# Graph convolutions on one core: node features as two 32-bit parts instead of three bf16 parts, edge counts stored as bytes and widened on chip

## The reference: what is computed

```
def _gcn_conv(x, src, dst, W, b, n_nodes):
    h = x @ W
    ...                       # self loops are added to src, dst as s, d
    deg = segment_sum(ones, d)
    dis = where(deg > 0, rsqrt(deg), 0.0)
    msg = h[s] * (dis[s] * dis[d])[:, None]
    return segment_sum(msg, d) + b

h = relu(batch_norm(gcn_conv(h, W1, b1)))
h = relu(batch_norm(gcn_conv(h, W2, b2)))
h = relu(gcn_conv(h, W3, b3))
h = gcn_conv(h, W3, b3)
x = x + h
```

## Time and profile before

| | |
|---|---|
| time, median of 3 runs | 3986.09 us |
| span of the profiled execution | 3987.6 us |
| PE busy | 3679.6 us (92%), 21902 matmul records |
| DVE busy | 2167.3 us (54%) |
| ACT busy | 1880.8 us (47%) |
| POOL busy | 1505.2 us (38%) |
| moved by DMA | 560.45 MB |

### The profile page before, as it was taken

How to read it: one execution, slowest core, us unless ns; L and a number is a source line. 1 busy time by engine, 2 the same in 40 slices (tenths; PEclk the granted TensorE clock), 3 DMA queues, 4 the chain that set the end, 5 groups by cost and what they waited for, 6 DMA issues and landing times. The chain is left out here.

```text
span 3987.6 us, 61840 instructions
## 1 busy us (share of the span) xinstructions
PE 3679.6 (92%) x21902; PEld 2157.9 (54%) x21902; DVE 2167.3 (54%) x3396; ACT 1880.8 (47%) x5147; POOL 1505.2 (38%) x1605
## 2 busy tenths in 40 slices
PE   5899999999999999999985879999999999999999
PEld 3566666666666666666653544445444544454444
DVE  8788888888888888888874750002100210012000
ACT  4788888888888888888863660002000100011000
POOL 2677777777777777777760000000000000000000
PEclk8788888888888888888886989999999999999999
DMA  6443333333333333333334126665666566665665
GB/s 202 128 109 104 105 106 105 105 106 105 106 105 105 106 106 106 105 106 105 105 92 88 38 65 204 204 196 181 199 194 208 174 194 203 205 189 184 213 204 159
DMA packets 467250, 560.45 MB, mean 141 GB/s; under 512 B 45449, under 2 KB 411684, under 8 KB 466686
## 3 DMA queue, kind: packets, MB, share of 16 engines
q1 hardware_dynamic: 383558, 366.63, 30.4%
q0 software_dynamic: 51168, 107.68, 12.2%
q10 hardware_dynamic: 32248, 82.62, 5.6%
HBM read 455.16 MB, written 103.20 MB: 140 GB/s over the span
## 5 line engine op out<-in xcount | busy, mean ns | idle before, releaser
L900 POOL DMA_INDIRECT fts<-ft_tab,src_all x1568 | 1483.0, 946 | 478.0 <-issue 477.4
L2171 PE MATMUL cv_acc<-cv_cnt,cv_parts 128*128 128x512 bf16 (+1 forms) x7056 | 1431.3, 366 | 0.0
L2171 PEld LDWEIGHTS cv_acc<-cv_cnt,cv_parts 128*128 128x128 bf16 x7056 | 666.0, 98 | 761.7
L2006 DVE TENSOR_TENSOR cv_y<-cv_acc,dis_row 128x512 f32<-128x512 f32 (+1 forms) x52 | 34.4, 661 | 1355.1 <-PE cv_acc L2171 1326.5
L937 DVE TENSOR_TENSOR ohk<-iota_ps,key_cols 128x784 bf16<-128x784 f32 x784 | 724.9, 966 | 6.1
L1030 ACT ACTIVATE dist_l<-lo_iota,low 128x128 bf16<-128x128 f16 x1960 | 593.7, 388 | 18.6 <-ACT low L1025 0.8
L1189 PE MATMUL agg_ps<-terms,oh 128*64 128x141 f32 x2744 | 528.7, 364 | 25.6 <-DVE terms L974 25.0
L1189 PEld LDWEIGHTS agg_ps<-terms,oh 128*64 128x64 f32 x2744 | 458.1, 180 | 80.6 <-DVE terms L974 67.3
L1082 ACT CAST strip<-adj_ps 128x392 bf16<-128x392 f32 x784 | 372.2, 475 | 271.4 <-PE adj_ps L1133 239.2
L1133 PE MATMUL adj_ps<-ohk,ohl 128*128 128x196 bf16 x3136 | 431.2, 263 | 0.0
L951 DVE TENSOR_TENSOR prod<-ftd_ps,fts 128x780 f32<-128x780 f32 (+1 forms) x392 | 271.1, 692 | 220.5 <-DMA fts<-ft_tab,src_all 212.3
(11 more groups left out here) (261 smaller groups left out, 2919.9 us busy)
## 6 DMA issues: line engine op xcount, KB each, us to landing
cv_cnt<-adj SPq DMA_DIRECT2D x96, 2048.0 KB, 8.3
cv_cnt<-adj SPq DMA_DIRECT2D x48, 2176.0 KB, 8.6
adj<-strip ACTq DMA_DIRECT2D x196, 392.0 KB
fts<-ft_tab,src_all POOLq DMA_INDIRECT x1568
win<-ft_tab SPq DMA_DIRECT2D x196, 65.0 KB
agg_tab<-res SPq DMA_DIRECT2D x196, 35.2 KB
cv_cnt<-adj SPq DMA_DIRECT2D x8, 512.0 KB, 3.7
agg_tab<-zero_f SPq DMA_DIRECT2D x10, 352.5 KB
```

Source lines behind the costliest of these rows:

```text
L900: nc.gpsimd.indirect_dma_start(fts[u][:, k, :], None, ft_tab[:, :], bass.IndirectOffsetOnAxis(src_all[:, n, k:k + 1], 0)).then_inc(gathere ...
L2171: last = nc.tensor.matmul(a[:, 0:width], parts[:, r, b, :], cnt[q][:, 0:width // SUB, (b - b0) * SUB:(b - b0 + 1) * SUB], start=(b == 0 an ...
```

## The change

1. The features are kept as two parts of type `float32r`, a 32-bit format that TensorE multiplies with 12 significant bits, so two parts carry 24 bits. The stationary operand of a source block is loaded twice, and there are 98 matmuls a group instead of 147.
2. Both operands of a matmul have this type, so the counts too are needed as 32-bit numbers. They are stored in `adj` as bytes, loaded as bytes (chunks of 15, 18 and 16 blocks), and widened in SBUF: of each unit of three blocks VectorE widens two (one cast of 1024 elements) and ScalarE the third (one of 512), into a ring of four units, `cv_ring`; the 49th block has a tile of its own, `cv_rest`, which ScalarE fills. TensorE waits for both engines at each unit and gives a unit back by `unit_used`.
3. In the first phase the scaling moves from ScalarE to VectorE, two instructions a tile of seven blocks (`scaled`), and there is one subtraction (`low`) where `split` had four instructions. ScalarE keeps `rectify` and makes the high part (`high`).
4. SyncE loads a chunk when the widening engines have read the one before, no longer when TensorE has. The ring of the next layer's first units is widened ahead of the last `finish_group` of a layer.
5. The loops over groups are written out in all layers.

```diff
-    adj = dram("adj", (NS, P, STRIP), BF16)
+    adj = dram("adj", (NS, P, STRIP), U8)
...
-        strip = sb("strip", [P, 2, NT, NA, HALF], BF16, c)
+        strip = sb("strip", [P, 2, NT, NA, HALF], U8, c)
...
+    UB = 3
+    UNITS = NT // UB
+    RING = 4
-        parts = sb("cv_parts", [P, 3, NT, D], BF16, c)
-        cnt = [g["cv_cnt0"]] + [sb(f"cv_cnt{q}", [P, SPG, CMAX * SUB], BF16, c) for q in (1, 2)]
+        parts = sb("cv_parts", [P, 2, NT, D], F32R, c)
+        cnt = [g["cv_cnt0"]] + [sb(f"cv_cnt{q}", [P, SPG, CHUNKS[q][1] * SUB], U8, c) for q in (1, 2)]
+        ring = sb("cv_ring", [P, RING, UB, GRP], F32R, c)
+        rest = sb("cv_rest", [P, GRP], F32R, c)
...
@@ SyncE
-                            sp.wait_ge(cnt_used[q], n + 1)
+                            if n:
+                                sp.wait_ge(s["wide_v"], unit_no(n - 1, (b0 + m) // UB))
+                                sp.wait_ge(s["wide_s"], (n - 1) * (UNITS + 1) + -(-(b0 + m) // UB))
...
@@ VectorE
+            def widen(n, u):
+                b = u * UB
+                dve.wait_ge(cnt_in[chunk_of(b)], 16 * (n + 1))
+                wait(dve, s["unit_used"], unit_no(n, u) - RING + 1)
+                src, view = widened(n, b, UB - 1)
+                nc.vector.tensor_copy(view(ring[:, u % RING, 0:UB - 1, :]), src).then_inc(s["wide_v"], 1)
...
+                    for i in range(1, NGA):
+                        for u in range(UNITS):
+                            if u == RING:
+                                finish_group(i - 1)
+                                if l == L - 1 and i >= 2:
+                                    add_rows(i - 2)
+                            widen(l * NGA + i, u)
+                    if l < L - 1:
+                        for u in range(RING):
+                            widen((l + 1) * NGA, u)
+                    finish_group(NGR)
...
@@ ScalarE
+            def widen(n, u):
+                b = u * UB + UB - 1
+                act.wait_ge(cnt_in[chunk_of(b)], 16 * (n + 1))
+                wait(act, s["unit_used"], unit_no(n, u) - RING + 1)
+                src, view = widened(n, b, 1)
+                nc.scalar.copy(view(ring[:, u % RING, UB - 1:UB, :]), src).then_inc(s["wide_s"], 1)
...
@@ TensorE
-                        for r in range(3):
-                            last = nc.tensor.matmul(a[:, 0:width], parts[:, r, b, :],
-                                                    cnt[q][:, 0:width // SUB, (b - b0) * SUB:(b - b0 + 1) * SUB],
-                                                    start=(b == 0 and r == 0), stop=(b == NT - 1 and r == 2))
+            def add_block(n, b):
+                u, w = b // UB, width(n % NGA)
+                if u < UNITS:
+                    if b % UB == 0:
+                        pe.wait_ge(s["wide_v"], unit_no(n, u) + 1)
+                    if b % UB == UB - 1:
+                        pe.wait_ge(s["wide_s"], n * (UNITS + 1) + u + 1)
+                    counts = ring[:, u % RING, b % UB, 0:w]
+                else:
+                    pe.wait_ge(s["wide_s"], (n + 1) * (UNITS + 1))
+                    counts = rest[:, 0:w]
+                for r in range(2):
+                    last = nc.tensor.matmul(acc[n % 2][:, 0:w], parts[:, r, b, :], counts,
+                                            start=(b == 0 and r == 0), stop=(b == NT - 1 and r == 1))
```

More of the change, by code:

```diff
@@ L7 @@
 BF16 = mybir.dt.bfloat16
+F32R = mybir.dt.float32r
+U8 = mybir.dt.uint8
 FP16 = mybir.dt.float16
@@ L2013, in _ @@
-                with dve.If(flag):
+                    dve.wait_ge(s["w_ps"], n + 1)
+                    if n >= 2:
+                        dve.wait_ge(s["high"], n - 1)
+                        dve.wait_ge(s["low"], n - 1)
+                    for b1 in range(0, w, 4):
+                        m = min(4, w - b1)
+                        last = nc.vector.tensor_tensor(
+                            hs[k % 2][:, b1:b1 + m, :], w_ps[k % 2][:, b1 // 4, 0:m * D].rearrange("p (b d) -> p b d", d=D),
+                            dis_col[:, b0 + b1:b0 + b1 + m].unsqueeze(2).to_broadcast([P, m, D]), ALU.mult)
@@ L2015, in _ @@
+                with dve.If(flag):
+                    scaled(0)
+                    for k in range(NW):
+                        if k + 1 < NW:
+                            scaled(k + 1)
+                        low(k)
+                    settle(dve, s["tick"])
                     with dve.Fori(0, NT) as k:
@@ L2063, in add_rows @@
                     def add_rows(n):
-                        w = GRP // P if n < NGR else LW // P
+                        w = width(n) // P
                         dve.wait_ge(s["out_ps"], n + 1)
@@ L2136, in _, with high, last_layer @@
-                in_turn(rectify, scaled)
+                def high(k):
+                    n, (b0, w) = l * NW + k, TILES[k]
+                    act.wait_ge(s["hs"], n + 1)
+                    nc.scalar.copy(parts[:, 0, b0:b0 + w, :], hs[k % 2][:, 0:w, :]).then_inc(s["high"], 1)
+                with act.If(flag):
+                    act.wait_ge(s["ready"], l + 1)
+                    for k in range(2):
+                        rectify(k)
+                    for k in range(NW):
+                        if k + 2 < NW:
+                            rectify(k + 2)
+                        high(k)
+                    if l == L - 1:
+                        act.wait_ge(s["y"], 2 * 7 + 2)
+                        act.sem_inc(s["out_ps"], 2)
+                        def last_layer(k, u):
+                            act.wait_ge(s["out_ps"], k + 1)
+                            nc.scalar.copy(stage[u][:].rearrange("f b p -> f (b p)"), hT[:, ds(k * BW, BW)]
+                                           ).then_inc(s["staged"], 1)
+                        with act.Fori(0, NB // 2) as m:
+                            for u in range(2):
+                                last_layer(2 * m + u, u)
+                        last_layer(NB - 1, 0)
@@ new lines, in _ @@
+                with act.Else():
+                    if l == 0:
+                        for u in range(RING):
+                            widen(0, u)
+                    act.wait_ge(s["ready"], l + 1)
+                    for k in range(2):
+                        rectify(k)
+                    for k in range(NW):
+                        if k + 2 < NW:
+                            rectify(k + 2)
+                        high(k)
+                        if k:
+                            for u in units_after(k - 1):
+                                widen(l * NGA, u)
+                    for u in units_after(NW - 1):
+                        widen(l * NGA, u)
+                    widen_rest(l * NGA)
+                    for i in range(1, NGA):
+                        for u in range(UNITS):
+                            widen(l * NGA + i, u)
+                        widen_rest(l * NGA + i)
+                    if l < L - 1:
+                        for u in range(RING):
+                            widen((l + 1) * NGA, u)
@@ L2176, in first_group, with group @@
+            def group(n):
+                wait(pe, acc_read, n - 1)
+                for b in range(NT):
+                    add_block(n, b)
             def first_group(l, k):
-                pe.wait_ge(s["split"], l * NW + k + 3)
+                if k == 0:
+                    wait(pe, acc_read, l * NGA - 1)
+                pe.wait_ge(s["low"], l * NW + k + 1)
                 for b in range(TILES[k][0], sum(TILES[k])):
-                    q = max(i for i in range(3) if CHUNKS[i][0] <= b)
-                    b0, m = CHUNKS[q]
-                    if b == b0:
-                        pe.wait_ge(cnt_in[q], (l * NGA + 1) * 16)
-                    for r in range(3):
-                        last = nc.tensor.matmul(acc[0][:], parts[:, r, b, :],
-                                                cnt[q][:, :, (b - b0) * SUB:(b - b0 + 1) * SUB],
-                                                start=(b == 0 and r == 0), stop=(b == NT - 1 and r == 2))
-                    if b == b0 + m - 1:
-                        last.then_inc(cnt_used[q], 1)
@@ L2218, in _ @@
                         settle(pe, s["tick_pe"])
-                        for r in range(3):
-                            last = nc.tensor.matmul(acc[0][:, 0:P], rows[:, r, :], oh[:], start=(r == 0), stop=(r == 2))
+                        for r in range(2):
+                            last = nc.tensor.matmul(acc[0][:, 0:P], rows[:, r, :], oh[:], start=(r == 0), stop=(r == 1))
                         last.then_inc(s["part_ps"], 1)
@@ L2247, in turn_rows @@
                             pe.wait_ge(s["sum"], n - 1)
-                        for b in range(w):
+                        for b in range(width(n) // P):
                             last = nc.tensor.transpose(w_ps[n % 2][:, 0, b * P:(b + 1) * P],
```

233 lines of the change are left out of this document (96 added, 137 removed).

## The result

| | before | after |
|---|---|---|
| median of 4 runs, same chip | 3986.83 us | 3559.27 us (3557.39 to 3560.38) |
| ratio | | 0.8924 (95%: 0.8912 to 0.8937) |
| profiled execution, span | 3987.6 us | 3557.1 us |

Faster by 428 us, where 495 was forecast (3491 us). The time is inside the range (3470 to 3580), and only 5 us from the time of a rival, VectorE as the bound (3564 us), so the number alone decides nothing. The trace does.

What follows compares the result with a forecast made beforehand. TensorE's matmul count times their distance was taken to bound the convolutions, gathers the attention stage. Middle groups -465, first groups -42, boundaries +10, layer 1 start +2.5 make -495 us: 3986 to 3491 us, range 3470 to 3580.

Steps and rivals of the forecast that it cites:

- VectorE as the bound: Rival, convolution groups: byte casts at the two-operand rate, 22.1 us a group on VectorE against 21.2; 3564 us, 24%.
- The mechanism: Convolutions: matmul count times distance is the time; 98 for 147 saves 10.57 us a group, -465 us in middle groups.
- The conditions under which a group fits: Middle groups: VectorE 13.4 us, ScalarE 10.5 us, ring returns and loads (6.2 us a chunk) fit within 21.2 us.
- two cycles a column: Rival, convolution matmuls: TensorE reads 32-bit columns at the f32 instruction's rate, 0.434 us a matmul; 4527 us, 9%.
- full f32: Rival, convolution matmuls: the type runs as two full f32 instructions, 85 us a group; over 6500 us, 2%.
- Bare weight loads: Rival, convolution matmuls: weight loads come out from under them, 0.216 + 0.19 us each, 39.8 us a group; 4386 us, 2%.
- The case that came true: Likeliest case, whole kernel: TensorE stays the bound of the convolutions; 3491 us, own range 3474 to 3525, 60%.
- the distance: Convolution matmuls of 512 columns: one instruction at one column a cycle, 0.216 us as for bf16, 21.2 us a group.
- The last group: Each layer's group of 128 columns: bounds 5.5 and 10.9 us, taken as 8.2 us, no gain.
- The boundary: Between layers: next layer's casts delay finish_group until 3.3 us after the sums are ready; +10 us for three.
- The starts of the layers: Start of each layer: shorter by a few instructions, at most 1.5 us each, not counted; layer 1 separately +2.5 us.
- the total for what is not a phase: Outside the phases: three boundaries, +10 us, and ScalarE's widening ahead of layer 1, +2.5 us; +12.5 us.

Runs made afterwards that it cites:

- experiment 1: Changed kernel with four layer 1 groups altered: 256 + 256 columns, 384 + 128, 320 + 192, and full f32; 3627.0 us.
- experiment 4: Changed kernel with VectorE widening each unit twice, first into a scratch tile as bf16; 3618.03 us, ratio 0.9078 to the kernel before.
- experiment 2: Changed kernel with FP16 in place of float32r for parts, ring and rest (22 bits); 3495.76 us, ratio 0.8769 to the kernel before.
- experiment 3: Changed kernel with TensorE's 98 unrolled matmuls in the skipped branch put back into a loop; 3542.45 us, ratio 0.8884 to the kernel before.
- experiment 9: Changed kernel with two layer 1 groups using 64 columns of the stationary part, or 64 partitions, for most source blocks; 3559.38 us.
- experiment 8: Changed kernel (float32r) with a loop in the skipped branch and the next layer's four casts moved into its first phase; 3541.11 us, ratio 0.8885.
- experiment 7: Changed kernel with FP16 parts, a loop in the skipped branch and the next layer's four casts moved into its first phase; 3469.78 us, ratio 0.8710.

## Why the prediction was right, and what it mis-sized

**The mechanism was right.** 98 matmuls for 147 on the engine that bounds the convolutions, one column a cycle, TensorE in the chain, the widening hidden. The conditions under which a group fits held with their numbers: casts of 0.693 and 0.623 us, chunks landing in 5.5 to 6.2 us, DMA share 0.52 to 0.54 for 0.55, attention unchanged. Of the rivals, two cycles a column (0.434 us) and full f32 (0.868) are refuted by the 0.227 us, full f32 besides by the 83.9 us of experiment 1. Bare weight loads (0.41 us) are refuted as well: 188 ns of load lie within the 227. On VectorE as the bound, experiment 4 decides.

That the range holds the time is in part luck. The case that came true had a range of its own, 3474 to 3525 us, and 3559 lies above it; the stated range reaches to 3580 only for the sake of the VectorE rival, which did not happen.

**The failed step is the distance.** "I take one instruction at one column a cycle, 0.216 us" took over the whole bf16 distance, the columns and what stands beside them. The columns were right; what stands beside them is 13.3 ns for float32r (512 and 256 columns, experiment 1) and 2.5 for bf16. In numbers: 48 groups x (22.26 - 21.16) = 53 us of the 68 that are missing. The forecast had a range for its likeliest case up to 3525 and in it no term for this; the bounds it had set (0.216 and 0.434) were right, and the lower one was taken without room above it. The Trainium skill (TensorE: Matmul & The Clock Gate, Wait — 56ns, not 53.3ns?) gives a fixed part of about 2.5 ns a matmul at the high clock. The bf16 and FP16 traces agree, 215.8 - 213.3; the float32r traces don't, with 13.3, and the measurement decides.

**The last group** was put at 8.2 us, with 10.9 as the upper bound. The upper bound is what happened (10.91 us): 0.111 us for 128 columns, as in the earlier trace rows. 4 x 2.7 = +11 us. The forecast's reason, the longer 32-bit weight load, fits: loads and matmuls both start 111 to 112 ns apart there, and FP16, with loads of 98 ns, has its narrow matmuls 56 ns apart. It is not shown apart from the type. Weight load and product of 32-bit type at this width were both in the rows of before; the bound nearest to the same type should have been the value.

**The boundary** was mis-sized by way of the last group: VectorE came when forecast, but the sums were ready 2.7 us later. +3.3 us each forecast, +0.44 measured, and with the short last group of FP16 it was 3.7, 3.9 and 4.7 us (experiment 2).

**The starts of the layers** were not costed ("shorter by a few instructions"). Beyond the 2.2 us that layer 1 begins later (2.5 forecast) they grew by 9.6 us, and most of that is the unrolled code in the branch that is never entered: 8.8 us of stops behind the 14th product and once in layer 2, by experiment 3. The diff and the order of the instructions show it; I had read the skipped branch as no work. So the total for what is not a phase came out near the forecast (+13.1 for +12.5) from other parts than the forecast's.

Altogether: +53 for the distance and +11 for the last groups give the 64 us that the phases miss, and with them the profiled 430.5 us for the forecast's 495. The medians lie 3 us closer together than the two profiled executions.

**How close the VectorE rival was.** Its own price, 22.1 us a group, is below the 22.26 that TensorE really takes. So even a cast at half the speed would hardly have lengthened a middle group. By the rival's own terms it would have added 0.44 us in each of 11 groups of the last layer, about 3 us in each first group (36.4 against 33.2) and up to 9 us at the boundaries and the start, some 25 us in all (an estimate), and not the 73 that set it apart in the forecast. That 3559 is so near to 3564 says nothing for it: the rival was summed on TensorE's forecast distance, which was too short. What tells the two apart is the mean time of a cast and the idle time in front of it.

## What to carry to other kernels

Where a type is new to a kernel, split the known distance into its columns and what is fixed: the columns may carry over and the fixed part not, and it is paid once for each matmul. At one column a cycle the choice among types is the count of matmuls times 0.216 (16-bit) or 0.227 us (float32r), and a stream of narrow matmuls of a 32-bit type (128 columns) stands at 0.111 us each. When a change brings two things, price them apart: here the bytes and the widening alone made the kernel slower by 0.6%, and with FP16 they could be left out. Look too at the code that a change writes out in branches that are never entered.

## What the runs showed of the hardware that I had not expected

- A float32r matmul comes every columns / 2.4 + 13.3 ns at full clock: 226.7 ns for 512, 119.9 for 256; a stream of 128 columns comes every 111 ns, and so do its weight loads. The fixed part doesn't shrink with a shorter weight load (134 ns for 188, experiment 9).
- VectorE's cast records of 0.69 us can overlap: four in a row take 2.70 us at the boundary, 0.67 from start to start, and in experiment 4 they start 0.61 and 0.72 us apart in turn. For a bound by throughput the start-to-start distance counts, not the duration.
- 98 matmuls in a branch that is jumped over cost TensorE 4.15 us of idle time at one start and 1.0 to 1.3 us at each of the others, always at the jump, and about 10 us over the four starts. The profile calls only the first of them "issue" and puts the others down to whoever released last.
- The first products of a layer can run at half clock. Granted clock 0.50 is the 1.2 GHz level; the first fourteen products of layer 4 take 3.3 us after the change, most of them at that level. This is the busy time by stretch, first of after, then of before:

```profile
3254.50:3257.80 3.30, 3.28 (x14) 3.03 (x14) 0.42 (x1) 1.79 (x3) 0.00 (x0) 0.53 0.54 129
```

```profile
3574.80:3577.00 2.20, 1.99 (x14) 1.69 (x14) 0.37 (x1) 1.99 (x5) 0.00 (x0) 1.00 1.10 348
```

TensorE had idled 1.96 us before them in the one and 1.52 in the other. But in experiment 8 it idled 1.52 us and the first products of layer 4 ran at 0.50 as well, so the idle time by itself isn't the cause. And in experiment 7 it idled 1.52 us and they ran at 1.00. It stays open, and 1 us or more a layer hangs on it (3.28 us busy for 14 products against 1.99).
